# Sharing the squaring of key tiles between ScalarE and GpSimd: one ScalarE tile in sixteen instead of one in eight

## What is computed

```python
Q, K, V = (proj(Wq, bq), proj(Wk, bk), proj(Wv, bv))
S = jnp.einsum('bhnd,bhmd->bhnm', Q, K) / dh ** 0.5
W_tau = jax.nn.softmax(S, axis=-1)
W_sigma = 1.0 / ((1.0 + jnp.abs(S) / b_) ** 2 + t_ ** 2)
W_sigma = W_sigma / W_sigma.sum(axis=-1, keepdims=True)
tau = jnp.einsum('bhnm,bhmd->bhnd', W_tau, V)
sigma = jnp.einsum('bhnm,bhmd->bhnd', W_sigma, V)
f = 0.5 * tau + 0.5 * sigma
```

## Time and profile before

| | us |
|---|---|
| median of 3 runs | 2055.33 |
| lowest and highest of them | 2053.5, 2062.61 |
| the profiled execution, its own time | 2054.09 |
| its span in the trace | 2052.3 |

### The profile page before, as it was taken

How to read it: one execution, slowest core, us unless ns; L and a number is a source line. 1 busy time by engine, 2 the same in 40 slices (tenths; PEclk the granted TensorE clock), 3 DMA queues, 4 the chain that set the end, 5 groups by cost and what they waited for, 6 DMA issues and landing times. The chain is left out here.

```text
span 2052.3 us, 26693 instructions
## 1 busy us (share of the span) xinstructions
PE 1578.5 (77%) x8579; PEld 562.9 (27%) x8579; DVE 1738.2 (85%) x3742; ACT 1631.2 (79%) x1406; POOL 1406.9 (69%) x962
## 2 busy tenths in 40 slices
PE   2587787777878878778878887778777587899966
PEld 1122222222222222222222222222222144366655
DVE  3889999997999999879999999999998278755556
ACT  2689999998999999989999999999999411122243
POOL 2889889987999989788998989988998001000000
PEclk7799999999999999989999999999999888877788
DMA  4000000001000000010000000000000000000001
GB/s 113 27 28 13 13 14 17 13 13 31 25 13 13 13 16 15 9 40 13 18 13 13 13 15 16 12 13 13 18 13 7 1 0 1 1 1 1 0 1 42
DMA packets 32490, 33.11 MB, mean 16 GB/s; under 512 B 5657, under 2 KB 23136, under 8 KB 32352
## 3 DMA queue, kind: packets, MB, share of 16 engines
q1 hardware_dynamic: 31056, 31.06, 5.0%
q10 hardware_dynamic: 1296, 0.35, 0.1%
HBM read 22.74 MB, written 8.39 MB: 15 GB/s over the span
## 5 line engine op out<-in xcount | busy, mean ns | idle before, releaser
L879 POOL TENSOR_TENSOR sigma_weights<-grown 128x1024 f32<-128x1024 f32 x448 | 845.6, 1893 | 0.0
L792 ACT ACTIVATE tau_weights<-ps_tau 128x1024 f32<-128x1024 f32 x512 | 740.1, 1446 | 29.6 <-PE ps_tau L424 29.5
L573 DVE TENSOR_SCALAR sigma_weights<-ps_sig 128x512 int32<-128x512 int32 x1024 | 693.4, 677 | 81.3 <-PE ps_sig L415 80.3
L852 POOL TENSOR_SCALAR grown<-sigma_weights,kernel_shape 128x1024 f32<-128x1024 f32 x448 | 501.3, 1119 | 196.8 <-DVE sigma_weights L573 196.7
L778 ACT ACTIVATE sigma_weights<-sigma_weights,kernel_shape 128x2048 f32<-128x2048 f32 x256 | 621.0, 2426 | 0.0
L582 DVE TENSOR_TENSOR running_max<-ps_sig,running_max 128x512 f32<-128x512 f32 x896 | 606.0, 676 | 0.0
L787 ACT ACTIVATE sigma_weights<-sigma_weights 128x2048 f32<-128x2048 f32 x256 | 598.4, 2338 | 0.0
L466 PE MATMUL ps_acc<-sigma_weights,v_heads 128*9 128x512 f32 x2048 | 534.6, 601 | 0.0
L466 PE MATMUL ps_acc<-tau_weights,v_heads 128*9 128x512 f32 x2048 | 533.1, 600 | 0.4 <-DVE sums L599 0.3
L424 PE MATMUL ps_tau<-q_operand,k_operand 128*128 128x512 bf16 x1024 | 310.5, 385 | 262.7 <-ACT tau_weights L792 256.2
L415 PE MATMUL ps_sig<-q_operand,k_operand 96*128 96x512 bf16 x1024 | 400.6, 391 | 67.0 <-DVE running_max L582 41.3
(11 more groups left out here) (169 smaller groups left out, 1459.8 us busy)
## 6 DMA issues: line engine op xcount, KB each, us to landing
q_operand<-q_parts SPq DMA_DIRECT2D x192, 48.0 KB
k_operand<-k_parts SPq DMA_DIRECT2D x64, 144.0 KB
q_parts<-parts SPq DMA_DIRECT2D x24, 128.0 KB, 2.3
k_parts<-parts SPq DMA_DIRECT2D x24, 128.0 KB, 2.3
x_res<-in_L_attn_x SPq DMA_DIRECT2D x8, 256.0 KB, 5.3
q_operand<-max_rows SPq DMA_DIRECT2D x128, 2.0 KB
out<-x_res SPq DMA_DIRECT2D x4, 512.0 KB, 3.2
experts<-in_L_ffn_expert_w SPq DMA_DIRECT2D x1, 512.0 KB
```

Source lines behind the costliest of these rows:

```text
L573: dve.tensor_scalar(sig[:, g % SIG_RING, cols].bitcast(I32), ps_sig[:, half, :].bitcast(I32), SIGN_OFF, None, ALU.bitwise_and).then_inc(ma ...
L792: act.activation(tau[:, g % TAU_RING, :], ps_tau[:, :, :].rearrange("p h q -> p (h q)"), ACT.Exp, scale=float(DH) ** -0.5).then_inc(tau_do ...
L852: pool.tensor_scalar(grown[:, g % GROWN_RING, :], sig[:, g % SIG_RING, :], 1.0, shape[:, g // TB % H, 0:1], ALU.mult, ALU.add).then_inc(gr ...
L879: pool.tensor_tensor(sig[:, g % SIG_RING, :], t, t, ALU.mult).then_inc(sq_ready, 1)
```

## The change

ScalarE squares tile 2 of the odd heads only. Tile 2 of the even heads goes through `grow` and the product on GpSimd as all other tiles do. The constants `WHOLE` and `OF` now describe a cycle of 16 tiles, in which tile 10 is ScalarE's, and the counts that the waits use follow from them.

```diff
-WHOLE = 2
+WHOLE, OF = TB + 2, 2 * TB
...
 def pooled(tiles):
-    return tiles - (tiles + TB - 1 - WHOLE) // TB
+    return tiles - (tiles + OF - 1 - WHOLE) // OF
...
-                if c % (TB // CHUNK) == WHOLE // CHUNK:
-                    act.wait_ge(whole_ready, CHUNK * c // TB + 1)
+                if c % (OF // CHUNK) == WHOLE // CHUNK:
+                    act.wait_ge(whole_ready, CHUNK * c // OF + 1)
...
-                if (g - LOG_LAG + 1) % TB == WHOLE and 0 <= g - LOG_LAG + 1 < TILES:
+                if (g - LOG_LAG + 1) % OF == WHOLE and 0 <= g - LOG_LAG + 1 < TILES:
                     square_whole(g - LOG_LAG + 1)
...
-                if g + 1 < TILES and (g + 1) % TB != WHOLE:
+                if g + 1 < TILES and (g + 1) % OF != WHOLE:
                     grow(g + 1)
                 beside.upto(g)
-                if g % TB == WHOLE:
+                if g % OF == WHOLE:
                     continue
```

## The result

The changed kernel takes 2030.22 us (median of four runs, 2029.09 to 2031.54) against 2055.51 us for the kernel before (four runs, 2053.5 to 2062.61). The ratio is 0.9871, with a 95% interval of 0.9847 to 0.9895: 25 us faster. The forecast was 2029.0. The profiled execution took 2030.23 us, with a span of 2028.4.

A forecast was written before the change was run, and what follows sets the result against it. ScalarE was taken to set the pace at 23.10 us a head, VectorE 1.1 us behind. The terms -27.0 - 2.1 + 3.3 = -25.8 us gave 2029 us on the scale of the runs, range 2026 to 2033 (0.60).

The forecast's parts named there:

- The pace is ScalarE's: Steady heads: ScalarE sets the pace, even heads fall from 23.10 to 22.06 us; 26 x 1.04 = 27.0 us saved.
- VectorE spends tile 7's wait: Steady heads: VectorE, floor 22.0 us, spends its 0.37 us wait in tile 7, so even heads take 22.06, not 22.37.
- C: Rival: GpSimd bounds each even head at 23.7 us, its lag not carried to the odd one; 2078 us, chance 0.06.
- the 0.09: VectorE's 0.09 us wait at the turn of a steady head, put down to ScalarE's square and expected to go without it.
- GpSimd's tiles are free, and the lag comes back: Steady pairs: GpSimd's 44.4 us fit ScalarE's 45.16; the even head's 1.6 lag is covered before the logarithm; cost nothing.
- the 3.33: GpSimd's time per tile in us, estimated from a reference page; the change would then lose 3.8 us a pair.
- Heads 16 and 32, 2.1 us saved: Even heads inside the projections: the square leaves the chain ahead of ScalarE's copy `h_turned`, saving 2 x 1.04 us.
- The `grow` ahead of low(3), 3.3 us lost: Heads 2, 18, 34: `grow` delays low(3), the stores and the next keys' load; TensorE waits 1.09 us longer each.
- A: Rival: VectorE inherits the pace, even heads take 22.37 us and save 0.73 each; 2037.5 us, chance 0.13.
- B: Rival: GpSimd reaches low(0) and low(1) late in the transitions, 8.9 us lost on top; 2038 us, chance 0.08 (alone or with A).
- D: Rival: no effect, ScalarE's fullness is an artefact of overlapping records, pace stays 23.10; 2055 to 2059 us, chance 0.06.
- E: Rival: more gain, nothing lost at low(3) or the transitions shift well; 2024 to 2026 us, chance 0.07.

The follow-up runs named there:

- nobody_even: Changed kernel without GpSimd's extra tiles: tile 2 of the even heads squared by no engine, 32 tiles unsquared; 2026.95 us, 0.9859 of the kernel before.
- nobody_all: Changed kernel with tile 2 of all heads squared by no engine, 64 tiles unsquared; 2000.1 us, 0.9721 of the kernel before.
- all_gpsimd: Changed kernel with every tile squared on GpSimd and none on ScalarE; 2085.06 us, 1.0137 of the kernel before.
- lows_back: Changed kernel with low(2) and low(3) due half a slot earlier on GpSimd, each ahead of the `grow` again; 2026.31 us, 0.9849 of the kernel before.
- all_lows_early: Changed kernel with low(2) and low(3) back to back and early on GpSimd, and low(0) and low(1) back to back too; 2008.58 us, 0.9766.
- one_in_twenty: Changed kernel with one ScalarE square in 20 tiles instead of 16; 2023.07 us, 0.9839 of the kernel before.
- low3_early: Changed kernel with low(2) and low(3) back to back on GpSimd, ahead of tile 1's `grow` and product in heads 2, 18, 34; 2016.16 us, 0.9803.

## Why the prediction was right, step by step

**The pace is ScalarE's.** Shown. The changed kernel and nobody_even both run 22.07 and 23.11, and the 26 even heads brought 26.6 us of the 27.0 forecast (1.02 each, for 1.04).

**VectorE spends tile 7's wait.** Right, and it was the step with the most at stake short of C (19 instead of 27 us). VectorE's short waits in tile 7 and behind it are gone wherever a turn without a square went before, and stand, 0.37 in tile 7, where one with a square did: the odd heads have none, the even ones keep theirs. That holds for the 0.09 too, which the prediction had put down to the square beside it: at the turn without a square it is still there (1445.09 to 1445.78, 0.69 for 0.60), and at the other it is gone. It never carried weight in the sum. No wait of ScalarE for `ps_tau` stands in a steady head. nobody_all shows that there was no such floor.

**GpSimd's tiles are free, and the lag comes back.** Right in time, a little off in size: 0.73 us of waits a pair are left (forecast 0.76), but the slack before the logarithm fell to 3.3 us where I had said near 4. The product ends 8.2 us after its magnitude instead of 7.1. That is the 1.1 I named. The other 0.8 the forecast left out: the logarithm, with the square ahead of it gone, starts 11.5 us after that magnitude instead of 12.3. all_gpsimd confirms the price of 2.96 a tile, not the 3.33 that the prediction weighed and set aside, as the bound of a head.

**Heads 16 and 32, 2.1 us saved.** The heads fell from 32.42 to 31.38 us and from 33.38 to 32.68, together 1.74. But head 17 took 31.40 us instead of 30.73, so 0.7 of it was lost again one head later. nobody_even has the same 31.38 and 31.40, so this isn't GpSimd's extra tile. It stands in one wait of ScalarE for tau scores, 1.97 us for 1.32, which is 1.40 in lows_back's head 17 (30.82 us); the prediction had no term for it, and what sets it isn't shown. Single traces scatter here: head 32 took 31.66 in nobody_even, 31.37 in lows_back and 33.23 in all_lows_early.

**The `grow` ahead of low(3), 3.3 us lost.** The place and the 1.1 us were right: 9.04 for 7.93, and 7.94 when undone. The step from there to the head was too simple. TensorE's waits for the keys of heads 3, 19 and 35 grew from 3.78, 2.55 and 3.46 us to 5.75, 3.68 and 4.45, that is 2.0, 1.1 and 1.0. The forecast said 1.09 each. Part of the growth was the load itself, which took 5.28, 4.98 and 5.79 us from issue to the first scores instead of 4.83, 4.38 and 5.28. And a wait of 1.1 us more wasn't 1.1 us more of head, because of the second wait, the clock's, for which the prediction had no term. ScalarE's second wait went from 0.51, 1.27 and 0.99 us in heads 2, 18 and 34 to none, none and 1.38. So head 18 stayed at 26.6, and the other two grew by 1.3 and 1.5, near what the two waits add up to: 2.7 us for the 3.3 forecast. Each transition ends within 0.8 us of its forecast, in part because such differences cancel: in heads 14-19 the loss of 1.1 that was forecast for head 18 didn't come, and the 0.7 of head 17 came in its place. The three together came to +1.7 us, forecast +1.2. lows_back ran 3.9 us below the changed kernel, in line with the 3.3, though by heads this is in part luck with loads and clock: in its trace heads 2 and 34 are 0.9 and 1.9 us shorter, and head 18, where the order was read, is 0.1 longer.

**The later blocks at nothing.** +1.1 us in these traces, within their spread.

Of the rivals, A is refuted by nobody_all. B did not come: low(1) starts 10.4, 11.0 and 11.2 us behind the second magnitude of tile 3 in heads 1, 17 and 33, where it was 10.4, 11.0 and 11.9 before. C is real but only where no odd head follows, D would have shown 23.1 in even heads, and E (2024 to 2026) is about where lows_back came out. What I had not seen is that the transitions, where I looked only for the change's own 1.2 us, held another 21.6 us, nearly as much as the whole change brought.

## What to carry to other kernels

When engines pass work through queues, take each one's own work per cycle from start-to-start distances, over as many heads as the lag needs to come back. The largest sum is the pace, and an engine may be over it in one head if it is under it in the next and the queue's room is larger than the lag. Then look at what the moved work now stands ahead of: one `grow` of 1.1 us ahead of an instruction that starts a chain of stores and a load went with 2.7 us in three places here. The instructions that start such chains are the first to put early; here that was worth nearly as much as the rebalancing.

## What the runs showed of the hardware

- GpSimd and VectorE didn't slow each other with the instructions of this kernel. With GpSimd busy 197.1 us of 200 instead of 179.0, the VectorE magnitude took 674 ns on average, as the group below shows (677 before), and GpSimd's tile 2.96 us up to its full 200.00 in all_gpsimd. In the page of the changed kernel:

```profile
L573 DVE TENSOR_SCALAR sigma_weights<-ps_sig 128x512 int32<-128x512 int32 x1024 | 690.6, 674 | 62.8 <-PE ps_sig L415 62.3
```

- A ScalarE record's length isn't its cost. The tau exponential is 1.02 us long after a wait (518.14) and 1.66 in steady running (1441.91), while the next instruction starts 0.92 and 0.91 us behind it.
- Seven kernels (before, after, nobody_even, nobody_all, all_gpsimd, lows_back, one_in_twenty) have three waits of TensorE for keys each, 1.9 to 6.1 us long. Around the end of each the clock was at 0.50, and it came back 3.0 to 8.4 us after that end (515.8 to 518.9 in the changed kernel, 515.1 to 521.2 in lows_back). ScalarE's second wait went with it: at most 0.4 us where the clock was back within 3.7 us, 0.3 to 1.0 at 4.4 to 5.1, 0.8 to 1.4 at 5.7 to 6.0, 2.5 to 2.7 at 7.8 to 8.4. With low3_early's keys in time in head 18 the clock stayed at 1.00.
- The load of the keys of heads 3, 19 and 35, where TensorE waited for it, varied from 4.3 to 5.8 us between issue and the first scores, with nothing changed about it.
